# C_LAG from 3 to 2: where GpSimd's C products stand in its queue, in a selective-scan kernel on one core

## The reference

```
def _L0_xattn_ref(hidden_states, z, ...):            # hidden_states (4,512,256), z = layernorm(x)
    x  = silu(causal_conv4(in_proj(hidden_states)))  # (4, 512 channels, 512 positions)
    dt_low, Bm, Cm = split(x_proj(x))                # ranks 16, 16, 16
    dt = softplus(dt_proj(dt_low) + dt_proj_b)
    def step(state, inp):                            # 512 positions, 16 states per channel
        state = state * exp(d[..., None] * A) + (d * u)[..., None] * b[:, None, :]
        y = einsum('bdn,bn->bd', state, c)
    y = (y + D * x) * silu(z)
x = x + _L0_xattn_ref(ctx_1024, layernorm(x), ...)
x = x + (layernorm(x) @ sum_r factors[r] / sqrt(8) + bias)
```

## Time and profile before

| | us |
|---|---|
| median of 3 runs | 494.79 (494.32 to 496.35) |
| the profiled execution | 493.95 |
| its span | 492.1 |

### The profile page before, as it was taken

The page is one execution under the profiler, slowest core; times in us unless marked ns, Lnnn a source line. Parts: engine busy times, 40 slices in busy tenths (PEclk is TensorE's granted clock), DMA queues, the critical chain, the costliest instruction groups (busy, mean ns, idle before and its releaser), DMA issues.

```text
span 492.1 us, 4146 instructions
## 1 busy us (share of the span) xinstructions
PE 427.1 (87%) x1058; PEld 181.4 (37%) x1066; DVE 466.6 (95%) x364; ACT 349.6 (71%) x625; POOL 451.1 (92%) x236
## 2 busy tenths in 40 slices
PE   9749897999787969889978789879889797979997
PEld 5213342434333423433424234333334243434432
DVE  4899899999999999999999999999999999999995
ACT  2787665978569768797788868798688885643432
POOL 4369998989899999999999899999999999999992
PEclk9978999999998989999999989999999998999999
DMA  5799743437992000100693000000395000000002
GB/s 188 256 357 351 191 81 76 83 69 217 271 365 87 0 0 0 46 20 1 226 414 113 1 1 21 0 21 2 122 385 225 1 21 21 22 23 21 0 0 85
DMA packets 17872, 53.96 MB, mean 110 GB/s; under 512 B 2725, under 2 KB 3237, under 8 KB 16825
## 3 DMA queue, kind: packets, MB, share of 16 engines
q1 hardware_dynamic: 16696, 45.31, 25.4%
q0 software_dynamic: 1152, 8.39, 8.3%
HBM read 49.24 MB, written 4.46 MB: 109 GB/s over the span
## 4 chain that ended last, share of the span: by engine, by line
POOL 27%; DVE 26%; issue 19%; PE 13%; ACT 9%; DMA 4%; SPq 2%; DVEq 0%; POOLq 0%; ACTq 0%
POOL h L1128 18%; DVE dA L977 13%; POOL h L1121 6%; PE y L521 5%; DVE h L977 5%; DMA b_rep<-bc_scratch 4%; PE work L514 3%; DVE h L983 3%; ACT dA L796 2%; DVE acc L934 2%; POOL dtu L1114 1%; SPq L343 1%; ACT gate L690 1%; PE work L516 1%; POOL fsum L1154 1%
## 5 line engine op out<-in xcount | busy, mean ns | idle before, releaser
L1128 POOL TENSOR_TENSOR h<-b_rep,dtu 128x1024 f32<-128x1024 f32 x127 | 301.9, 2436 | 12.8 <-DVE dtu L1084 9.9
L521 PE MATMUL y<-h,ident 128*128 128x512 f32 x508 | 245.3, 619 | 52.0 <-DVE h L983 50.9
L796 ACT ACTIVATE dA<-dt,a_neg 128x512 f32<-128x512 f32 x256 | 165.8, 680 | 83.5 <-DVE h L983 73.6
L977 DVE TENSOR_TENSOR_SCAN dA<-dA,h 128x1024 f32<-128x1024 f32 x84 | 191.8, 2283 | 2.5 <-ACT dA L796 2.5
L521 PEld LDWEIGHTS y<-h,ident 128*128 128x128 f32 x508 | 93.4, 193 | 186.0 <-issue 103.6
L1121 POOL TENSOR_TENSOR h<-h,c_rep 128x1024 f32<-128x1024 f32 x44 | 104.7, 2379 | 9.1 <-DVE h L977 9.1
L977 DVE TENSOR_TENSOR_SCAN h<-dA,h 128x1024 f32<-128x1024 f32 x44 | 100.3, 2279 | 2.7 <-ACT dA L796 2.7
L983 DVE TENSOR_TENSOR h<-dA,c_rep 128x1024 f32<-128x1024 f32 x83 | 101.0, 1217 | 1.4
L410 PE MATMUL work<-ctx_sb,w_in 128*128 128x512 f32 x60 | 29.4, 618 | 1.4 <-DVE x L1019 1.2
L514 PE MATMUL work<-fsum,xnT 128*128 128x512 f32 x64 | 29.4, 602 | 0.0
L934 DVE SCALAR_TENSOR_TENSOR acc<-work,chan,acc 128x511 f32<-128x511 f32 (+2 forms) x30 | 21.5, 729 | 6.1 <-ACT acc L655 5.9
(11 more groups left out here) (137 smaller groups left out, 424.2 us busy)
## 6 DMA issues: line engine op xcount, KB each, us to landing
b_rep<-bc_scratch SPq DMA_DIRECT2D x32, 512.0 KB, 9.5
c_rep<-bc_scratch SPq DMA_DIRECT2D x32, 512.0 KB, 8.8
fsum<-factors POOLq DMA_DIRECT2D x8, 1024.0 KB, 8.2
x<-x SPq DMA_DIRECT2D x4, 1024.0 KB, 7.9
out<-x SPq DMA_DIRECT2D x16, 256.0 KB, 2.0
ctx_sb<-ctxT SPq DMA_DIRECT2D x3, 512.0 KB, 4.5
ctx_sb<-ctxT SPq DMA_DIRECT2D x2, 256.0 KB, 3.7
w_in<-w_inT SPq DMA_DIRECT2D x1, 384.0 KB, 4.8
```

Source lines behind the costliest of these rows:

```text
L521: mm = pe.matmul(y[:], ident[:], h[:, (s * PAIRS + j) % H_RING, i, :], start=False, stop=(j == sum_order(s)[-1] and i == 1))
L796: act.activation(dA[:, j % 2, i, :], dt[:, k % 2, :], ACT.Exp, scale=a_neg[:, k, 2 * j + i:2 * j + i + 1]).then_inc(exp_done, 1)
L977: dve.tensor_tensor_scan(pair if on_pool(s * PAIRS + j) else decay, decay, pair, 0.0, ALU.mult, ALU.add).then_inc(scanned, 1)
L1128: pool.tensor_tensor(h[:, (s * PAIRS + j) % H_RING], b_rep[:, j], dtu[:, k % 2, :].unsqueeze(1).to_broadcast([P, 2, L]), ALU.mult).then_in ...
```

## The change

One constant. A C product on POOL stands behind the B product two pairs on, where before it stood behind the one three pairs on. All places that use the constant are in POOL's program: the two lines of the loop above, and the loop behind the last step, which makes the C products that are left over (none is: the last of POOL's is pair 15.4).

```
-C_LAG = 3
+C_LAG = 2
```

## The result

| | before | changed |
|---|---|---|
| median of 20 runs, us | 495.48 | 498.54 |
| ratio, 95% interval | | 1.0054 (1.0028 to 1.0081) |
| profiled execution, us | 493.95 | 496.99 |
| its span, us | 492.1 | 495.2 |

What follows compares the result with a forecast made beforehand. VectorE was taken to set the end, with GpSimd nearly full and without slack in two stretches. Terms +0.92 + 0.56 - 0.68 = +0.80 us on the median 494.79 gave 495.6 us, range 493.6 to 497.9.

Steps and rivals of the forecast that it cites:

- What bounds the kernel: Whole kernel: VectorE sets the end, busy 440.25 of 451.10 us; GpSimd is nearly full, without slack in two stretches.
- Steps 0 to 4: B products come later but the lead suffices, tightest at pair 2.1 with 0.6 to 1.0 us left; cost nothing.
- Steps 5 and 6: GpSimd runs 2.35 us late from pair 4.4 on, so the scan of 5.7 starts 0.92 us late.
- Steps 7 to 12: GpSimd's waits for scans pin it to VectorE again; no B product is late, cost 0.
- Steps 13 to 15: GpSimd is late after pair 12.4, 1.26 us of it left at the end; scan of 15.7 0.56 us late.
- The end: Last sum: TensorE gets the C product of 15.4 no later, past a B product, and takes up 0.68 us.
- The base: The median of the kernel before, 494.79 us, to which the predicted 0.80 us was added.
- rival C: TensorE's clock: one more half-clock stretch beside a step's gate adds 1.65 us, giving 497.2, two 498.9; chance 0.08.
- a half clock in a new place: Sign, anywhere in the trace: a stretch of half TensorE clock at a new place would show the forecast wrong.
- Rival A: No product is late in either full stretch; only the 0.68 us gained at the end remains, 494.1 us; chance 0.17.
- B: Handoff from GpSimd to VectorE is long, some 0.9 us, at scans 5.7, 15.7, 2.1, 3.1: 497.5 to 497.8; chance 0.11.
- D: Faster: TensorE's 1.1 and 3.5 us of waits for GpSimd's C products all go, 490.2 us; chance 0.06.

Runs made afterwards that it cites:

- fill2: The changed kernel plus filler on TensorE (products with a zero matrix in its waits): median 495.07 us, ratio 1.0007 to the kernel before.
- fill_last: The kernel before plus the filler of fill2, and only the C product of pair 15.4 ahead of the B product of 15.7: 492.41 us, ratio 0.9940.
- b3: A further trace of the kernel before, nothing changed: 494.03 us.

## Why the prediction was wrong

- *What bounds the kernel*: right. VectorE sets the end, GpSimd has no idle time in two stretches.
- *Steps 0 to 4, nothing*: right. The B product of 2.1 had 0.75 us of lead left (0.6 to 1.0 forecast).
- *Steps 5 and 6, 0.92 us*: right, 1.12. GpSimd came 2.37 us late (2.35 forecast). The handoff is 0.10 in place of 0.05 (the prediction took PE's for VectorE's), and the B product of 5.7 ended 0.15 later than I had it (194.84 against 195.87 - 1.18).
- *Steps 7 to 12, nothing*: right.
- *Steps 13 to 15, 0.56 us*: 0.25 at 14.3, nothing at 15.5 and 15.7. Before GpSimd could be late there, VectorE had been held up 1.7 us by TensorE at 14.7 and 15.1, which hid it. Where it isn't held up, as in fill2, the lateness is 1.9 and above my term.
- *The end, -0.68*: -0.53.
- These terms together: forecast +0.80, in the trace 1.12 + 0.25 - 0.53 = +0.84. That they agree so well is in part luck: the term of steps 13 to 15 was twice too large and at other pairs, and that of the end depends on the trace.
- *The base*: the 0.80 was put on a median of 3 runs, 494.79; that of 20 is 495.48. So 0.7 of the 2.9 us by which 495.6 was missed is the base and not the change.
- **The step that failed** is what is not among the terms: that TensorE's clock stays as it is, at no cost (the sum has no term for it; rival C has it). I followed GpSimd's lateness to VectorE's scans and took every wait behind them as shifted by as much. TensorE's wait ahead of the last sum of step 5 is not shifted but longer, since it starts with work that is not late and ends with a scan that is. In four of the five traces with this lateness the clock fell behind that wait, and the fall at the sum of 5.7 cost 1.66 us. The prediction had named a half clock in a new place as a sign of being wrong, and 199.4 is one. Rival C had such a fall and this price (1.65 for one, 498.9 for two; measured 1.66, and 1.70 for the one at 14.3), with a chance of 0.08 and with the argument against it that TensorE doesn't wait for the products that move later. It doesn't wait for B products; it waits for the sum's own product, and that one comes behind a scan that waited for one.
- *Rival A* falls, products are late. *B* falls, the handoff is 0.10. *D* falls: TensorE's waits for C products fell from 4.6 to about 2 us, and no scan came sooner by it; the end is the one place that gained.
- What stays open: whether the change brings the fall at 14.3, and how much of the 2.7 us is the falls. By the traces it would be 0.84 plus 3/4 of 1.66 plus 3/4 of 1.7, 3.4 us; four traces of each are few, and the timed intervals (1.4 to 4.0 us for the change as a whole, 1.0007 against 0.9949 with filler) don't separate the parts.

## What to carry over

When two engines are nearly full, moving an instruction ahead in one's queue is paid by the instruction behind it: look for the stretch where that queue has no idle time, and add one instruction's length to every handoff after the last wait. Then look at a third engine that waits there. A wait that begins with work on time and ends with work that is late gets longer, and on TensorE it can cost more than itself (here 0.9 us more wait, and 1.66 us behind it). Filler in its waits, with the gain at the end taken alone (fill_last), was the fastest version here, 0.6% under the kernel before (0.9940, 0.9913 to 0.9967).

## What the runs showed of the hardware that I had not expected

- The time of this kernel varies by 11 us between executions (493.2 to 504.5), and much of that goes with TensorE's granted clock: in that batch and the one ahead of it the kernel before ran 493.1 to 494.8 us at 0.971, and 496.4 to 504.5 at 0.952 to 0.959. It is no strict rule: at 0.972 four runs took 496.0 to 497.6. With filler the range was 3 to 5 us.
- The same number of falls isn't the same loss. At 0.965 and 0.966 most runs of the kernel before took 493.3 to 494.5 us and most of the changed one 497 to 499. In b3 falls at 80.0 and 134.6 us shift no scan; those at 329.1 and 441.8 cost 1.1 and 1.7.
- A fall isn't settled by the wait ahead of it: behind a wait of 3.23 us at 438.8 the clock stayed in the first trace of the kernel before, behind one of 1.98 at 284.1 it fell.
- From the end of a GpSimd product to the scan that waits for it the traces show 0.10 us (once 0.11), at every late place (5.5, 5.6, 5.7, 14.3; in the other runs 6.0, 14.0, 14.1, 15.5 and 15.7 too), where to TensorE they show 0.05, from ScalarE's decays to a scan 0.03 and from a scan to GpSimd 0.08.
